# Two-layer graph network: one tile of every eighth group fetched row by row, and a second pass with 15 groups made and four gathered early

## Chip, cores and metric

The kernel runs on one core of a Trainium2 chip. The metric is the device time of one execution in microseconds, the median of several runs. Six actors matter: TensorE (PE, with its weight loads PEld), VectorE (DVE), ScalarE (ACT), GpSimd (POOL), which issues gathers, SyncE (SP), which issues plain copies, and the 16 DMA engines that all of them share.

## What is computed

A graph of N = 6250 nodes with 96 features and E = 100000 edges sorted by destination. Two layers, each with a residual and a normalization:

```
h    = concat(x[src], edge_attr)                      # E x 128
msg  = gelu(h @ mW1 + mb1) @ mW2 + mb2
gate = sigmoid(gelu(h @ gW1 + gb1) @ gW2 + gb2)
agg  = segment_sum(msg * gate, dst, N)
x1   = layernorm(x + layernorm(x + mlp(concat(x, agg))) ...)
# layer 2 (GCN), deg = segment_sum(edge_weight, dst) + 1
norm = deg[src]**-0.5 * edge_weight * deg[dst]**-0.5
out  = segment_sum((x1 @ W)[src] * norm, dst, N) + self loop + b
return layernorm(x1 + out)
```

## The kernel before

**Tiling.** Edges are cut into tiles of 128 and groups of TG = 8 tiles (1024 edges); there are NG = 98 groups. Nodes are cut into NB = 49 blocks of 128. As the edges are sorted by destination, a group's destinations lie in a window of W = 80 nodes, so its sums are one accumulated product with a one-hot of 80 columns (`ps_win`), which VectorE adds into `acc1`.

**Pass 1** (`step1` on each engine, one step a group). GpSimd gathers x[src] of a tile with one indirect DMA (L430), eight a group, into a ring of eight `rows` buffers; it waits for `s_xt`, the transposes of the group eight earlier. TensorE transposes the eight tiles (L520, `transposes`), ScalarE copies them out (L769), TensorE multiplies (L543, L546), ScalarE applies Gelu (L784), VectorE makes gate, values and one-hot (L1034 to L1126), TensorE sums the window (L493). Every second step also finishes one node block: update, both normalizations, and x_nat[:, b], the scaled input of layer 2, written by VectorE (L1203) and sent to the table `x1s_table` in HBM by ScalarE's queue (L854).

**Dense groups.** Gathering is dear on GpSimd, so in pass 2 only some groups are gathered. For the others TensorE multiplies x_nat, which is in SBUF, with a matrix B of 128 x (49 blocks x 12 nodes) for each of the group's eight tiles: B[i, (block, node)] holds the weight of each edge whose source is row i of the block. B is itself the product of two one-hots made by VectorE (`hots`, L1133 and L1137). 40 groups are dense: 24 are *stored* (kind P): their B is made in pass 1 beside the other work, two tiles each step (`pair_hot`, `pair_cells` L571, `pair_copy` L824), and SyncE stores the pair to `b_table` in HBM (L406, 96 pairs of 600 KB) and loads it again in pass 2 (L393). The pair's buffer is one of two: ScalarE's copy waits on `s_stored` for the store two pairs earlier. 16 groups are *built* (kind B): their B is made in pass 2 (`dense2` on VectorE, `cells2` L625 on TensorE, L829 on ScalarE).

**Pass 2** (`usual2`). It runs in turns, one dense group a turn. `second_pass` (L54) says which gathered groups are added in the same turn: one in a stored turn, two in a built one, one more in three turns, and a 41st turn with the last two gathered groups alone. On TensorE a stored turn q is: sums over blocks 0 to 5 (L645), turn-over of the sums of q-1 (L715, if that was a stored one), blocks to 11, placing of q-1's sums (L721), blocks to 32, gathered groups (L730), node matmuls of the output parts ready after q-1 (L692), the other blocks. A built turn is: 16 cells with turn-over, placing and outputs among them, then gathered groups, then sums over 49 blocks (L642). VectorE in turn q: the node one-hot (L1242), one-hot and weights of each gathered group (L1034, L1043), the one-hots of the next group if it is a built one (two halves of L1133 x4 and L1137), the output parts ready after q-1 (`block2`, L1294 to L1309), then the window additions of turn q (L1281), for which it waits for the placing, in TensorE's turn q+1. Node blocks are finished in parts of three; a part is ready when the last group that adds to it has been added. GpSimd's gathers of pass 2 wait for all of `x1s_table` (`s_xsw`) and then for the window addition of the group eight earlier (`s_acc2`).

**Order around the change.** Each engine runs its program in order. A function `run_pass` (L290) is called twice by TensorE, ScalarE and VectorE: each time the engine reads one number and branches to the usual case or to a general one. In pass 1 SyncE's queue holds only the pair stores, behind the loads of the start (2.4 MB each for x_t and x_nat).

## Time and profile before

| | us |
|---|---|
| median of 3 runs (1638.93 to 1643.31) | 1641.12 |
| the profiled execution | 1641.43 |
| its span | 1639.6 |
| TensorE busy | 1435.3 (88%) |
| VectorE busy | 1143.4 (70%) |
| GpSimd busy | 1178.4 (72%) |
| ScalarE busy | 559.8 (34%) |

Pass 1 takes about the first 1008 us of the span, pass 2 the rest. Busy counts time inside instructions; a queue that issues without pause (GpSimd: 0.94 us in a gather and 0.30 us between two) shows 75% busy and is full. The order in time and the waits say more than the shares.

### The profile page before, as it was taken

The numbers are of one execution on the slowest core, as the hardware profiler recorded it, in microseconds if no ns is written. First come the engines' busy times: TensorE is split into PE (matmuls) and PEld (weight loads), VectorE is DVE, ScalarE is ACT, GpSimd is POOL, SyncE is SP. The second block draws the span as 40 slices with busy tenths as digits, with TensorE's granted clock in tenths as the row PEclk, the third lists the DMA queues.
The fourth block names the chain that finished last, engine by engine and source line by source line (L and its number), as shares of the span: only waits on it lengthen the run. The fifth ranks groups of instructions, "written<-read, shape, count | busy, mean of one in ns | idle before, by whom it ended". The sixth has DMA issues, their size and how long they took to land.

```text
span 1639.6 us, 31556 instructions
## 1 busy us (share of the span) xinstructions
PE 1435.3 (88%) x11180; PEld 1273.6 (78%) x11181; DVE 1143.4 (70%) x3201; ACT 559.8 (34%) x985; POOL 1178.4 (72%) x1257
## 2 busy tenths in 40 slices
PE   3526999999999999999999987899999999998996
PEld 2415878787878778787877776799998989887986
DVE  5314889888988888889888887444654556555543
ACT  1103545454544545454544443111111111212110
POOL 7777777777777777777777770677777777777771
PEclk8767999999999999999999999999999999999997
DMA  3423444344444444444444443454544435353530
GB/s 106 123 67 109 133 120 131 115 134 116 134 117 126 124 127 125 115 134 118 133 116 127 122 116 115 130 173 125 168 143 126 165 104 167 101 191 102 196 112 19
DMA packets 80039, 205.95 MB, mean 126 GB/s; under 512 B 39325, under 2 KB 40893, under 8 KB 76703
## 3 DMA queue, kind: packets, MB, share of 16 engines
q1 hardware_dynamic: 28688, 127.68, 20.5%
q0 software_dynamic: 39808, 61.22, 17.4%
q10 hardware_dynamic: 11376, 14.90, 3.1%
q8 instruction: 95, 1.56, 0.4%
q14 instruction: 72, 0.59, 0.1%
HBM read 139.91 MB, written 63.80 MB: 124 GB/s over the span
## 4 chain that ended last, share of the span: by engine, by line
DVE 37%; PE 34%; DVEq 14%; issue 7%; DMA 3%; another core or an unknown queue 2%; POOL 2%; ACT 1%; ACTq 0%; POOLq 0%
DVE shared L1137 8%; PE ps_bt L642 8%; PE ps_win L730 5%; PE ps_xt L645 5%; PE ps_hid L645 4%; DVE logit L1126 4%; DVE shared L1133 3%; DVE edges L1102 3%; DVEq L1125 3%; PE ps_hid L625 3%; PE ps_xt L625 3%; DVEq L1049 2%; DVE prod L1123 2%; DVEq L1100 2%
## 5 line engine op out<-in xcount | busy, mean ns | idle before, releaser
L430 POOL DMA_INDIRECT rows<-in_x_nat,idx x782 | 740.5, 947 | 243.0 <-issue 237.0
L430 POOL DMA_INDIRECT rows<-x1s_table,idx x462 | 436.0, 944 | 184.6 <-issue 139.9
L546 PE MATMUL ps_hid<-w,edges 128*128 128x192 f32 x1568 | 325.2, 331 | 0.0
L546 PEld LDWEIGHTS ps_hid<-w,edges 128*128 128x128 f32 x1568 | 272.2, 194 | 14.3 <-issue 1.3
L1137 DVE TENSOR_TENSOR shared<-cell,ps_fix 128x1200 f32<-128x1200 f32 (+1 forms) x128 | 218.3, 1706 | 0.0
L784 ACT ACTIVATE edges<-ps_hid 128x768 f32<-128x768 f32 x196 | 159.1, 812 | 172.1 <-PE ps_hid L546 171.1
L1281 DVE TENSOR_TENSOR acc<-acc,ps_win 96x80 f32 x98 | 22.9, 234 | 240.2 <-PE ps_win L721 217.0
L493 PE MATMUL ps_win<-hot,edges 128*98 128x80 f32 x1568 | 156.1, 254 | 28.7 <-DVE acc L1051 28.6
L493 PEld LDWEIGHTS ps_win<-hot,edges 128*98 128x98 f32 x1568 | 148.8, 170 | 40.8 <-DVE edges L1102 39.1
L520 PE MATMUL ps_xt<-ident,rows 128*96 128x128 f32 x784 | 108.9, 284 | 71.9 <-ACT shared L824 40.2
L520 PEld LDWEIGHTS ps_xt<-ident,rows 128*96 128x96 f32 x784 | 89.2, 131 | 87.1 <-ACT shared L824 50.4
L543 PE MATMUL ps_hid<-b_split,ones_b 128*128 128x384 bf16 x392 | 129.9, 331 | 7.6 <-DVE step L998 5.9
L824 ACT ACTIVATE shared<-ps_hid 128x600 f32<-128x600 f32 x96 | 64.4, 671 | 189.6 <-PE ps_hid L571 189.6
L1034 DVE TENSOR_TENSOR hot<-dst_rel,ps_fix 128x640 f32<-128x640 f32 x156 | 126.6, 811 | 0.1
L769 ACT ACTIVATE edges<-ps_xt 96x1024 f32<-96x1024 f32 x98 | 100.0, 1020 | 72.3 <-PE ps_xt L520 68.6
L571 PE MATMUL ps_xt<-shared 128*128 128x300 f32 x384 | 114.4, 421 | 4.3 <-DVE shared L1137 4.3
L571 PE MATMUL ps_hid<-shared 128*128 128x300 f32 x384 | 116.2, 425 | 0.9 <-ACT edges L784 0.9
L730 PE MATMUL ps_win<-hot,rows 128*96 128x80 f32 x928 | 95.5, 264 | 21.6 <-DVE hot L1043 19.9
L1133 DVE TENSOR_SCALAR shared<-ps_fix,src_low,weight 128x128 f32<-128x128 f32 x320 | 112.6, 401 | 1.9 <-issue 1.9
L730 PEld LDWEIGHTS ps_win<-hot,rows 128*96 128x96 f32 x928 | 92.2, 180 | 26.4 <-issue 24.9
L824 ACT ACTIVATE shared<-ps_xt 128x600 f32<-128x600 f32 x96 | 64.4, 671 | 118.1 <-DVE edges L1102 53.4
L1126 DVE TENSOR_REDUCE logit<-prod 128x8 f32<-128x768 f32 x98 | 93.4, 953 | 7.2
(157 smaller groups left out, 2241.8 us busy)
## 6 DMA issues: line engine op xcount, KB each, us to landing
b_table<-shared SPq DMA_DIRECT2D x96, 600.0 KB, 3.4
edges<-b_table SPq DMA_DIRECT2D x12, 2400.0 KB
wide<-b_table SPq DMA_DIRECT2D x12, 2400.0 KB
rows<-in_x_nat,idx POOLq DMA_INDIRECT x782, 2.7
edges<-in_edge_t ACTq DMA_DIRECT2D x96, 128.0 KB
rows<-x1s_table,idx POOLq DMA_INDIRECT x462
wide<-in_x_t SPq DMA_DIRECT2D x1, 2376.5 KB
out_nodes<-y SPq DMA_DIRECT2D x49, 48.0 KB
```

Source lines behind the costliest of these rows:

```text
L430: nc.gpsimd.indirect_dma_start(out=rows[slot][:, k, :], out_offset=None, in_=table, in_offset=bass.IndirectOffsetOnAxis(ap=idx[:, TG * g + ...
L493: mm = nc.tensor.matmul(ps_win[0:rws, 0:W], lhs[:, k, :], hot[u][:, k, :], start=(k == 0), stop=(k == TG - 1))
L520: mm = nc.tensor.transpose(ps_xt[m // 4][0:ND, P * (m % 4):P * (m % 4 + 1)], rows[v][:, m, :], ident[:, :])
L546: mm = nc.tensor.matmul(ps_hid[j][:, HC * q:HC * (q + 1)], feat[u][:, P * m:P * (m + 1)], w1[:, :], start=False, stop=(q == 1))
L571: mm = nc.tensor.matmul(ps_pair[i][:, m, 0:HW], pair_low[n % 2][:, i, :], pair_place[n % 2][:, 2 * i + m, :], start=True, stop=True)
L642: mm = nc.tensor.matmul(ps_bt[0:TW, 0:ND], unit_b[d % 2][:, TW * c:TW * (c + 1)], x_nat[:, c, :], start=(c == 0), stop=(c == NB - 1))
L645: mm = nc.tensor.matmul(raw_sums(d), x_nat[:, c, :], unit_b[d % 2].rearrange("p (k x) -> p k x", k=TG)[:, :, WD * c:WD * (c + 1)], start=( ...
L730: mm = nc.tensor.matmul(ps_win[0:ND, W * col:W * (col + 1)], rows[i % SLOTS][:, k, :], hot[i % 2][:, k, :], start=(k == 0), stop=(k == TG ...
L784: nc.scalar.activation(flat(hid[u][:, 4 * half:4 * half + 4, :]).rearrange("p (j c) -> p j c", j=2), ps_pair[1][:, :, 0:2 * HC], ACT.Gelu) ...
L1126: nc.vector.tensor_reduce(logit[u][:, :], prod[:, :, :], AX, ALU.add).then_inc(s_logit, 1)
L1133: nc.vector.tensor_scalar(low[:, i, :], places_ps[:, 0:P], src_low[:, TG * d + k:TG * d + k + 1], weight[:, TG * g + k:TG * g + k + 1], AL ...
L1137: return nc.vector.tensor_tensor(place, cells.to_broadcast(shape), places_ps.rearrange("p (o w) -> p o w", o=1).to_broadcast(shape), ALU.i ...
```

## The change

1. **Row fetches in pass 1.** In the groups 15, 23, ..., 95 (11 of them) the last tile isn't gathered by GpSimd. SyncE copies its 128 rows one at a time from x_nat in HBM into one of two buffers (`far`), with the row's number read from SBUF into a register (eight numbers a read): 16 rows after each of the first 88 pair stores. TensorE's transposes of these groups wait for `s_far` too.
2. **Early gathers.** SyncE also copies each of the first 43 finished node blocks to a second table `x1s_early`, whose 44th block is zeros. After pass 1's gathers GpSimd gathers the groups 1, 4, 6, 7 from it, with the source number cut off at the zero block. What these groups take from the last six blocks is computed as for a dense group, with 72 columns instead of 600 (`early_cells`, `early_sums`, `early_placed`), after the sums of the first two built turns.
3. **Turns.** One built site (group 44) becomes a gathered group: 39 turns, 15 built, 59 gathered groups (four of them early). The gathered groups of each turn come from a table `TAKES`; there is no 41st turn. In the last turn they follow all the sums, and turn-over and placing come after them.
4. **One branch.** `run` holds both passes inside one branch.

```diff
+LEFT_OUT = (18,)
+SITE = [i for i in range(len(SITES)) if i not in LEFT_OUT]
+EARLY = (1, 4, 6, 7)
+DONE_B = 43
+EARLY_IN = {BUILT[0]: (0, 1), BUILT[1]: (2, 3)}
+TAKES = (0, 0, 2, 2, 2, 1, 1, 2, 2, 2, 2, 2, 2, 2, 2, 0, 1, 1, 1, 1, 2, 2, 2, 0, 2, 1, 2, 0, 1, 2, 2, 1, 2, 2, 2, 2, 2, 2, 2)
+FAR = [SLOTS * k + FAR_V for k in range(1, ROUNDS)]
...
+            def far_rows(i, first, n, buf):
+                for r in range(first, first + n, FAR_LOAD):
+                    _, nodes = nc.values_load_multi_w_load_instructions(
+                        far_idx[i:i + 1, r:r + FAR_LOAD], engines=(mybir.EngineType.SP,), min_val=0, max_val=N - 1,
...
+                    for m, node in enumerate(nodes):
+                        sp.dma_start(far[buf][r + m:r + m + 1, :], t["x_nat"][ds(node, 1), :]).then_inc(s_far[buf], 16)
...
                     sp.dma_start(b_table[P * p:P * (p + 1), 2 * CELLS * v:2 * CELLS * (v + 1)], ready_b[n % 2]).then_inc(s_stored[n % 2], 16)
+                    b = n // 2 - LAG - 1
+                    if n % 2 == 0 and 0 <= b < DONE_B:
+                        sp.wait_ge(s_xs, b + 1)
+                        sp.dma_start(x1s_early[P * b:P * (b + 1), :], x_nat[:, b, :]).then_inc(s_early, 16)
+                    if n < SLOTS * len(FAR):
+                        i = n // SLOTS
+                        if n % SLOTS == 0 and i >= 2:
+                            sp.wait_ge(s_xt, FAR[i - 2] + 1)
+                        far_rows(i, FAR_ROWS * (n % SLOTS), FAR_ROWS, i % 2)
...
+                pool.wait_ge(s_early, 16 * DONE_B)
+                for i in range(NE):
+                    pool.wait_ge(s_xt, NG - SLOTS + i + 1)
+                    early_gathers(i)
                 pool.wait_ge(s_xt, NG)
...
+            def early_part(q, es):
+                for e in es:
+                    early_cells(e)
+                for e in es:
+                    early_sums(q, es, e)
+                early_placed(q, es)
...
-                        gathered_of(turn)
+                        if q < NTURN - 1:
+                            gathered_of(turn)
                         outputs(q - 1)
                         dense_sums(q, range(SUMS_AFTER, NB))
+                        if q == NTURN - 1:
+                            gathered_of(turn)
+                turn_over(NTURN - 1)
+                place_sums(NTURN - 1)
+                outputs(NTURN - 1)
```

On TensorE the node matmuls of a part (`block2`, L686) begin with `wait(pe, s_finr, b)`: the part before must have been read by VectorE.

Turns as both tables give them (kind, gathered groups, node blocks ready after the turn), where the prediction speaks of them:

```
before: 14 P 31 (13-15) | 15 P 33 | 16 B 35 37 || 19 P 43 (19-21) | 20 P 45 | 21 B 47 49
after:   4 P 2 9 (0, 1-3) | 5 P 11 | 6 B 13    || 18 P 44 (19-21) | 19 P 45 | 20 B 47 49
after:  33 P 79 81 (37-39) | 34 P 83 85 | 35 B 86 88 (40-42) | 36 P 90 91 | 37 B 93 95
```

## Rows read from the trace of the kernel before

**Rows 1.** Waits of GpSimd, whole span: us in total, times, longest.
```profile
POOL rows L430 <- issue: 376.9, 1237, 0.3
POOL rows L430 <- DMA x1s_table<-x_nat: 44.1, 1, 44.1
POOL rows L430 <- PE ps_xt L520: 3.7, 3, 3.1
```

**Rows 2.** Order in time (start, us, engine, line, operation, [idle before]): transposes, one gather.
```profile
147.55 1.04 PE L520 MATMUL ps_xt<-ident,rows 128*96 128x128 f32 x8
...
148.89 0.94 POOL L430 DMA_INDIRECT rows<-in_x_nat,idx  x1 [0.31 <-PE ps_xt L520]
...
901.23 1.04 PE L520 MATMUL ps_xt<-ident,rows 128*96 128x128 f32 x8
911.92 1.77 PE L520 MATMUL ps_xt<-ident,rows 128*96 128x128 f32 x8 [2.28 <-issue]
...
991.95 1.04 PE L520 MATMUL ps_xt<-ident,rows 128*96 128x128 f32 x8
```

**Rows 3.** Order in time: ScalarE's wait for the first pair store.
```profile
135.96 0.67 ACT L824 ACTIVATE shared<-ps_xt 128x600 f32<-128x600 f32 x1 [39.10 <-DMA b_table<-shared]
```

**Rows 4.** Order in time: SyncE's queue issues small loads at the start.
```profile
7.13 0.28 SPq L385 DMA_DIRECT2D mw<-in_mb  x1
7.46 0.31 SPq L385 DMA_DIRECT2D uw1x<-in_uW  x1
...
9.65 0.43 SPq L385 DMA_DIRECT2D ln_g<-in_ln_g  x1
```

**Rows 5.** Order in time, then the page's DMA issues (count, KB, us to landing).
```profile
494.33 0.67 ACT L824 ACTIVATE shared<-ps_xt 128x600 f32<-128x600 f32 x1 [0.39 <-PE ps_xt L571]
496.34 0.33 DVE L1203 TENSOR_SCALAR x_nat<-h_c,root,dinv 128x96 f32<-128x96 f32 x1
...
b_table<-shared SPq DMA_DIRECT2D x96, 600.0 KB, 3.4
```

**Rows 6.** Order in time: VectorE and TensorE at the switch of passes.
```profile
1030.43 1.36 DVE L1133 TENSOR_SCALAR shared<-ps_fix,src_low,weight 128x128 f32<-128x128 f32 x4 [1.91 <-issue]
1033.21 0.57 PE L645 MATMUL ps_xt<-edges,x_nat 128*96 128x96 f32 x4 [2.69 <-issue]
1035.45 0.80 PE L645 MATMUL ps_xt<-edges,x_nat 128*96 128x96 f32 x4 [1.67 <-issue]
```

**Rows 7.** Order in time: TensorE in a built turn and the stored turn after it.
```profile
1244.56 1.20 PE L625 MATMUL ps_xt<-shared 128*128 128x300 f32 x4
...
1255.82 4.49 PE L730 MATMUL ps_win<-hot,rows 128*96 128x80 f32 x32 [2.51 <-DVE hot L1043]
...
1268.52 1.69 PE L645 MATMUL ps_xt<-wide,x_nat 128*96 128x96 f32 x18
...
1274.13 1.51 PE L730 MATMUL ps_win<-hot,rows 128*96 128x80 f32 x16
...
1278.38 1.20 PE L625 MATMUL ps_hid<-shared 128*128 128x300 f32 x4
```

**Rows 8.** Order in time: VectorE beside the start of that built turn.
```profile
1242.60 1.35 DVE L1133 TENSOR_SCALAR shared<-ps_fix,src_low,weight 128x128 f32<-128x128 f32 x4
1243.88 2.64 DVE L1137 TENSOR_TENSOR shared<-cell,ps_fix 128x2400 f32<-128x2400 f32 x1
1246.62 0.77 DVE L1294 SCALAR_TENSOR_TENSOR h<-ps_bn,dinv,x1b 128x96 f32<-128x96 f32 x3
...
1253.24 0.23 DVE L1281 TENSOR_TENSOR acc<-acc,ps_win 96x80 f32 x1 [0.69 <-issue]
```

**Rows 9.** Waits of TensorE from 1050 us on: us in total, times, longest.
```profile
PE ps_win L730 <- DVE hot L1043: 19.9, 9, 4.4
```

**Rows 10.** Order in time: TensorE at the end.
```profile
1622.67 5.38 PE L730 MATMUL ps_win<-hot,rows 128*96 128x80 f32 x32 [4.44 <-DVE hot L1043]
1629.49 1.60 PE L692 MATMUL ps_bn<-w_gcn,agg_t 96*128 96x96 f32 x6 [1.45 <-ACT agg_t L868]
```

More of the change, by code:

```diff
@@ L42 @@
 STORED = [d for d in range(NTURN) if KIND[d] == "P"]
-GATHERED = [g for g in range(NG) if g not in DENSE]
-DT = NTURN * TG
+FIRST_BUILT = BUILT[0]
+EARLY = (1, 4, 6, 7)
+NE = len(EARLY)
+DONE_B = 43
+LATE_B = NB - DONE_B
+LATE_C = LATE_B * WD
+GATHERED = list(EARLY) + [g for g in range(NG) if g not in DENSE and g not in EARLY]
+DT0 = len(SITES) * TG
+DT = DT0 + NE * TG
 PAIRS = len(STORED) * TG // 2
@@ L64, in second_pass @@
     added = {g: q for q, turn in enumerate(turns) for g in turn}
+    whole = dict(place)
+    for q, es in EARLY_IN.items():
+        for g in [EARLY[e] for e in es]:
+            added[g], whole[g] = max(added[g], q), max(whole[g], place[turns[q][0]])
     parts = []
@@ L68, in second_pass @@
         needs = range(min(2 * (b + n - 1) + 3, NG))
-        parts.append((b, n, max(added[g] for g in needs), max(place[g] for g in needs) + 1))
+        parts.append((b, n, max(added[g] for g in needs), max(whole[g] for g in needs) + 1))
     return turns, place, parts
 TURNS2, PLACE, PARTS = second_pass()
-assert PAIR_AT + PAIRS == NG
+assert PAIR_AT + PAIRS == NG and not set(EARLY) & set(SITES)
+assert FIRST_BUILT == 1 and len(TURNS2[0]) == len(TURNS2[1]) == 1
 assert ND + ED == P and NB == TURNS and SLOTS % 2 == 0 and LEFT == 2
@@ L417, in end1, with early_gathers, gathers @@
                     outputs(q)
[L418 removed]
             sp.wait_ge(s_steer, 1)
             hard = sp.value_load(steer[0:1, 3 * NG:3 * NG + 1], min_val=0, max_val=NG * NW)
+            sp.wait_ge(s_far_idx, 16)
             with sp.If(hard < 1):
                 end1()
+            with sp.Else():
+                for i in range(len(FAR)):
+                    sp.wait_ge(s_xt, FAR[i] - SLOTS + 1)
+                    far_rows(i, 0, P, 0)
         @block.gpsimd
         def _(pool):
[L427 removed]
+            def early_gathers(i):
+                for k in range(TG):
+                    nc.gpsimd.indirect_dma_start(
+                        out=rows[slot_of(i)][:, k, :], out_offset=None, in_=x1s_early,
+                        in_offset=bass.IndirectOffsetOnAxis(ap=idx_early[:, TG * i + k:TG * i + k + 1], axis=0)).then_inc(
+                            s_rows2[i % SLOTS], 16)
+            def gathers(g, slot, table, rows_sem, n):
                 last = g == NG - 1
[L429 removed]
+                elsewhere = table is not x1s_table and g in FAR
+                for k in range(TG - (REST if last else 1 if elsewhere else 0)):
                     nc.gpsimd.indirect_dma_start(
@@ L1224, in end1 @@
                 block1([], last)
-            run_pass(dve, step1, lambda b: block1a(b, False), ahead=True, even=LAG + 1, end=end1, close=close1, finish=finish1)
             def step2(k, v, easy, b):
```

296 lines of the change are left out of this document (209 added, 87 removed).

## The prediction

> **What bounds the kernel now.** I read the waits first, then the order of time. GpSimd's waits [rows 1] say that its queue issues gathers end to end: 1237 gaps of 0.3 us between descriptors, one pause of 44.1 us at the switch between the passes, and almost nothing spent on TensorE (3.7 us in 3 waits). A queue that never stops looks like the bound. The question is whether anybody waits for it, and when.
>
> Pass 1. Read the starts of a group's eight transposes [rows 2]. Group 6's stand at 147.55 and group 88's at 901.23: 82 groups in 753.7 us, 9.19 us each. GpSimd needs 8 x 1.25 = 10.0 us for a group; it was eight groups ahead at 148.89, where its last wait for TensorE ends [rows 2], and loses 0.8 us a group. Its group 89 is issued by 148.89 + 76 x 10.0 = 908.9, and there TensorE waits for the first time (911.92, 2.28 us idle). From then on TensorE follows the gathers: group 97 at 991.95. So pass 1 has two bounds: TensorE and its partners to group 88, the gathers for the last nine groups only. Before group 6 there is a third: ScalarE stands 39.1 us for the first pair store, which lands behind the big loads on SyncE's queue [rows 3].
>
> Pass 2. GpSimd again runs through, but TensorE's waits name it nowhere. They name the one-hots: 19.9 us in nine waits for L1043 [rows 9]. One long wait stands in the rows of a built turn [rows 7]: cells from 1244.56, then nothing for 2.5 us until 1255.82. VectorE shows why [rows 8]: it ends the one-hots of this built group at 1246.5, then has an output part's three node blocks (1246.62 to 1253.2, 6.6 us with the value reads behind them), then window additions, and only then the hots that TensorE wants at 1253.3. This is the pattern of five such waits (2.51, 2.18, 2.78, 3.97, 3.06 us, 14.5 together): an output part became ready, the next turn is a stored one (short) and the one after it a built one. A sixth, 4.44 us, stands ahead of the last two gathered groups [rows 10]. After such a wait 32 matmuls take 4.49 us where a quick set takes 2.87 (twice the 16 of [rows 7] gives 2.7), so each costs 1.6 us more.
>
> **The change, part by part.**
>
> (a) Row fetches. 11 of the 782 gathers of pass 1 leave GpSimd, 11 x 1.25 = 13.75 us, all after its last wait, so all are kept. Group 97's rows, landing near 989, would land near 975. TensorE on its own rhythm gets to group 97 at 901.23 + 9 x 9.19 = 983.9, not 991.95. The gain is 8.0 us; the rest of the 13.75 is slack.
>
> (b) What pays for it: SyncE issues 11 x 128 = 1408 copies of one row, 16 after each pair store, with two register reads of eight numbers. Small copies on this queue stand in [rows 4]: one row to one partition takes 0.28 us and the next starts 0.33 us after it; a 128-partition copy takes 0.43 (0.48 with its gap). No row shows a copy with an address from a register, nor a register read on SyncE. Over two groups (18.4 us) SyncE has two pair stores (0.65), one early store (0.42), and 32 rows at c each. With c = 0.33 that is 11.7 us, at 0.48 16.4 us; it fills the 18.4 us at c = 0.54. I take c = 0.45, nearest to the one-row copies and with an allowance for the reads: 15.5 us, it fits. The new wait for s_xs on even groups stands ahead of 16 rows and the next pair store: pair copies end at 495.0, x_nat is written at 496.67 [rows 5], so 1.7 us of idle, inside the 3 us left. The next pair store may then be late by 1 to 2 us; a store lands in 3.4 us [rows 5] and its buffer is wanted a whole group later, so nobody waits. Cost 0, cover about 5 us of lateness. Priced outward: a little over c = 0.54 each extra 0.01 us costs 0.3 us per two groups, 44 times.
>
> The Trainium skill (DMA: Bandwidth & Descriptors, Rules for kernel authors) speaks against this edit: many small transfers should be coalesced, since under 64 KB one pays mostly overhead. The same page (Latency and other measured facts) puts the floor of a register read at about 600 ns; four of them in two groups would be 2.4 us, and with c = 0.33 for the copy alone, by estimate, SyncE would have 14.1 us of work: still inside.
>
> (c) The start. One load of row numbers, one store of zeros, some 25 small operations on VectorE, 0.1 to 0.2 us each. All lie ahead of the 39.1 us stall [rows 3] and vanish in it. Cost 0; without that cover up to 4 us.
>
> (d) The 43 early stores are SyncE's (in (b)). The four early groups (32 gathers, 40 us) fall in the 44.1 us pause of [rows 1]: GpSimd ends pass 1 near 972, the early ones near 1012, and the others start when x1s_table has landed. Free. They shorten GpSimd's pass 2, which nobody waits for: worth 0 as such.
>
> (e) One branch instead of two. At the switch VectorE idles 1.91 us on issue before its half of the first built group (1030.43) and TensorE 2.69 us before the rest of the sums (1033.21), then 1.67 us more (1035.45); the built group's cells follow that row's matmuls, near 1036 [rows 6]. With no second branch VectorE has the one-hots ready near 1032.5 (1028.5 + 1.36 + 2.64), and TensorE starts the cells then, near 1032.7. Gain 3.3 us (bounds 0 and 4.4).
>
> (f) Pass 2, TensorE. A built turn costs 8.7 us of cells and 8.4 us of sums, as 1244.56 to 1255.82 less the wait, and 1255.82 + 4.49 to 1268.52 with 0.2 us of overlap show [rows 7]; one goes: -17.1. One more gathered group comes: +1.4 (1.51 us for 16 matmuls at 1274.13, 1.35 net of the overlap). The early parts: for each of four groups 16 short matmuls (72 columns: 1.2 us scaled from the 16 of 80, 2.1 by the eight 128-column ones of [rows 2], 1.04 us), 12 of the sums (1.05 us by 8.4 for 98), one placing (0.2): 2.5 to 3.4. In each of two parts TensorE also waits for VectorE between first and second group (about 1.7 to 2), and for two copies of ScalarE (about 1). 8.2 us a part, 16.4 together (bounds 11 and 19).
>
> (g) Where the stalls go. I wrote out both turn tables and looked for the pattern. VectorE's terms from a turn's start: placing 2.35, additions 0.41 each, node 0.2, hots 1.6 each, one-hots of a built group 8.0 (twice 1.35 + 2.64), output part 6.6 [rows 8]. A stored turn takes TensorE 5.6 us to its gathered sums (1268.52 to 1274.13), 1.35 for each of n, 0.8 for an output part, 2.9 for the rest (1278.38 is the next turn) [rows 7]; a built one wants its first hot at 8.75. Check on before, with one gathered group in the stored turn: VectorE 2.35 + 0.8 + 0.2 + 1.6 + 8.0 + 6.6 = 19.55, TensorE 10.65; so VectorE is 8.9 into the built turn, plus two additions, node and hot 11.5, wait 2.8; measured 2.5, so I take 0.4 off each. In the new table the pattern stands before turns 20, 35 and 37: one wait of 2.5 and, with two gathered groups in the stored turn, two of 3.4; with 1.6 to 1.7 of slow matmuls each, 14.4 us. Turn 10 gives 0.5. And a new one: output parts 0 and 1 to 3 are both ready at turn 4. The second part's matmuls wait for VectorE to have read the first (s_finr), and VectorE gets there only after the built one-hots of turn 6: 2.35 + 1.2 + 0.2 + 1.6 + 8.0 + 0.9 = 14.2 after the start of turn 5, TensorE is there at 7.2. 7.0 us plus 1.7 slow. New stalls 23.6; old ones leave 14.5 + 5 x 1.6 = 22.5.
>
> (h) The end. The last two gathered groups now follow the sums directly; the 4.44 us wait and 2.5 us of slow matmuls go (5.38 for 2.87, [rows 10]): -6.9. Turn-over, its two copies, the placing and a third addition now stand between these sums and the last node matmuls: 4.0 us where 1.4 are (1628.05 to 1629.49), while 1.6 ahead of them go: +1.0.
>
> Sum: pass 1 -8.0, switch -3.3, pass 2: -17.1 + 1.4 + 16.4 + 23.6 - 22.5 - 6.9 + 1.0 = -4.1. Together -15.4, from the profiled execution's 1641.4 us (span 1639.6, 1.8 outside) to 1626; the median of the runs is 0.3 us less. Forecast 1626 us.
>
> **The rivals.**
> A, SyncE becomes the bound of pass 1, the one that ends slower. A copy with a computed address, and its part of the reads, costs more than 0.54 us. Then the pair stores come late, ScalarE waits for s_stored, and TensorE behind it. With a row priced as the dearest small copy (0.48) plus 0.1 for address and reads, c = 0.58: 1.1 + 18.6 = 19.7 against 18.4, 1.3 x 44 = 57 us, in all about 1683. For it: 84% of the queue's time is filled at c = 0.45, and no row has the form. Against: the one-row copies are the cheap ones. At the threshold the change turns from gain to loss within 0.02 us of c (0.015 x 32 x 44 = 21 us).
> B, GpSimd was the bound of pass 2 after all, and its relief counts in full: its 438 gathers start near 1022 and end at 1569, where before 462 from 1030.0 end at 1607.5; 38 us sooner, and the end follows: about 1603. For it: no pause in [rows 1], TensorE near 97% busy. Against: [rows 9].
> C, nothing comes through: TensorE's rhythm in pass 1 slows by 0.1 us a group, as SyncE's copies share issue and DMA rings with ScalarE's (8 us), and the early parts cost their upper bound or their waits bring the slow clock: 1640, between 1636 and 1646.
>
> **How the numbers follow.** Forecast and what lies near it (1608 to 1636): 0.62. A: 0.18. B: 0.07. C: 0.13. The bounds of (e), (f), (g) move the forecast by +-9 us. The low end is 1606, so that B is left out. The high end, 1650, takes in C and the mildest part of A; outside lie most of A and of B, some 2 in 10. About 0.3% (4.9 us) is what a measurement of this kernel can tell from no change. Faster by more: forecast and B, 0.69. Within: C but for 0.01, 0.12. Slower by more: A and that 0.01, 0.19.
>
> **What would show it.** (a) No wait of TensorE for rows after group 88, group 97's transposes near 984, and GpSimd's pass 1 ended near 972. (b) SyncE's row copies 0.3 to 0.45 us apart and ScalarE without waits for b_table; many such waits would be A. (e) Cells about 3.3 us nearer to the last stores. (f) Two parts of about 8 us. (g) One TensorE wait of 7 us before the node matmuls in turn 5, and three of 2.5 to 3.5 before turns 20, 35, 37's gathered sums. (h) No wait before the last gathered pair. I am wrong if the rhythm of 9.19 us moves, or if TensorE waits for rows in pass 2.

## The result and the profile after

The changed kernel takes **1687.3 us** (median of 4 runs, 1683.1 to 1692.4) against 1642.0 us (4 runs) of the kernel before. The ratio is 1.028, with a 95% interval of 1.025 to 1.031: slower by 45 us. The forecast was 1626 with a range of 1606 to 1650, so it was wrong in sign. What came is rival A, put at 0.18 and priced at 1683.

In some runs below every kernel, the kernel before included, takes half as long again, so a time that stands beside a kernel before of 2485 to 2516 us is compared with that one alone.

The profiled execution took 1692.4 us (span 1690.5), the longest of the four; before it was 1641.4 (1639.6). Read in the order in which the prediction read the kernel before, it says this.

Waits first (engine, line, waited for: us in total, times, longest). This is the view of rows 1 and 9, of the changed kernel:

```profile
ACT shared L949 <- DMA b_table<-shared: 178.2, 69, 38.0
PE ps_xt L609 <- ACT shared L949: 99.4, 57, 36.8
...
POOL rows L506 <- DMA x1s_table<-x_nat: 27.0, 1, 27.0
POOL rows L506 <- DVE acc L1473: 15.9, 6, 10.9
POOL rows L506 <- PE ps_xt L609: 9.3, 15, 5.0
```

ScalarE's copy of a pair's cells (L949) waited for a pair store once, 39.1 us, in the kernel before [rows 3]. Now it waits 69 times. The first wait is that old one (38.0 us); the other 68 share 140 us, some 2.1 each. TensorE stands behind it 57 times. GpSimd, which was to be relieved, now waits for TensorE more often than before [rows 1].

Then SyncE's queue, in order of time, over two groups:

```profile
480.41 0.36 SPq L461 DMA_DIRECT2D b_table<-shared  x1
480.83 0.42 SPq L465 DMA_DIRECT2D x1s_early<-x_nat  x1
483.56 7.35 SPq L455 DMA_DIRECT2D shared<-in_x_nat  x16
490.96 0.36 SPq L461 DMA_DIRECT2D b_table<-shared  x1
492.64 7.29 SPq L455 DMA_DIRECT2D shared<-in_x_nat  x16
499.98 0.36 SPq L461 DMA_DIRECT2D b_table<-shared  x1
```

From one even pair store to the next are 19.57 us (19.45 around 430 us), with no pause: each store is issued some 0.05 us after the last row copy. The gaps ahead of the row copies (2.3 us from the end of the early store to 483.56, 1.3 us from the end of the pair store to 492.64) are register reads; a third and a fourth read stand inside the batches of sixteen. Grouped by line (operation, count: ns least/median/most, first and last start):

```profile
L451 SPq TENSOR_LOAD <-shared x176: 562/943/2238, 133.1 to 987.6; - x176
L455 SPq FUSED_REGOPS  x1408: 37/37/48, 133.7 to 991.7; - x176
L455 SPq MOVE shared<-in_x_nat x1408: 29/29/38, 133.8 to 991.8; - x176
L455 SPq DMA_DIRECT2D shared<-in_x_nat x1408: 224/228/628, 133.9 to 991.8; - x176
```

The page's chain of work that ended last names the same queue, which had no part worth a word in it before: SPq has 47% of the span, of it L455 (the row copies) 25% and L451 (the reads) 11%.

TensorE's transposes (rows 2's view) and the stall of turn 5:

```profile
149.33 1.04 PE L609 MATMUL ps_xt<-ident,rows 128*96 128x128 f32 x8
...
1036.86 1.04 PE L609 MATMUL ps_xt<-ident,rows 128*96 128x128 f32 x8
...
1172.05 1.56 PE L779 MATMUL ps_bn<-w_gcn,agg_t 96*128 96x96 f32 x6 [6.09 <-DVE h L1486]
```

Group 6 to group 97 take 887.5 us, 9.75 us a group: half of SyncE's 19.5. Before, group 97 stood at 991.95 [rows 2], so **44.9 us of the loss are made in pass 1**. From group 97's transposes to the end of the span are 653.6 us, where the kernel before has 647.7: 6.0 more before rounding. The two are the whole difference of the spans (50.9). The 6.0 can't be laid to the change: a run below with the same pass 2 (one read of sixteen) has 645.9 us there.

### The profile page after: what moved, and what is told of

Read it like the earlier page. It is cut to its first block, busy times and chain, and to the rows that moved or that the text cites. A ratio compares the mean times of both kernels' runs of the same rounds, so it can differ in the third digit from the quotient of the medians.

```text
span 1690.5 us, 36100 instructions
## 1 busy us (share of the span) xinstructions
PE 1449.3 (86%) x11184; PEld 1282.5 (76%) x11185; DVE 1155.8 (68%) x3266; ACT 552.9 (33%) x986; POOL 1177.4 (70%) x1254
## 4 chain that ended last, share of the span: by engine, by line
SPq 47%; PE 29%; issue 13%; DVE 8%; DVEq 2%; DMA 1%; ACT 0%; ACTq 0%
SPq L455 25%; SPq L451 11%; PE ps_bt L731 7%; SPq L435 6%; PE ps_win L817 4%; PE ps_hid L734 4%; PE ps_xt L734 4%; PE ps_xt L714 3%; PE ps_hid L714 3%; SPq L461 2%; DVE shared L1289 2%; SPq L432 2%; SPq L465 1%; DVE shared L1285 1%; DMA edges<-b_table 1%
## 5 line engine op out<-in xcount | busy, mean ns | idle before, releaser
L506 POOL DMA_INDIRECT rows<-in_x_nat,idx x771 | 730.9, 948 | 241.8 <-issue 230.0
L506 POOL DMA_INDIRECT rows<-x1s_table,idx x438 | 414.2, 946 | 174.2 <-issue 131.4
L1289 DVE TENSOR_TENSOR shared<-cell,ps_fix 128x1200 f32<-128x1200 f32 (+1 forms) x126 | 213.0, 1691 | 0.0
L949 ACT ACTIVATE shared<-ps_xt 128x600 f32<-128x600 f32 x96 | 64.4, 671 | 198.2 <-DMA b_table<-shared 178.2
L949 ACT ACTIVATE shared<-ps_hid 128x600 f32<-128x600 f32 x96 | 64.4, 671 | 168.2 <-PE ps_hid L660 166.6
L1251 DVE TENSOR_SCALAR ps_fix<-squash 128x8 f32<-128x8 f32 x98 | 16.2, 165 | 129.8 <-ACT squash L928 128.5
L817 PEld LDWEIGHTS ps_win<-hot,rows 128*96 128x96 f32 x944 | 91.1, 175 | 17.7 <-issue 16.2
```

The lines of the kernel that those rows point to most:

```text
L506: nc.gpsimd.indirect_dma_start(out=rows[slot][:, k, :], out_offset=None, in_=table, in_offset=bass.IndirectOffsetOnAxis(ap=idx[:, TG * g + ...
L817: mm = nc.tensor.matmul(ps_win[0:ND, W * col:W * (col + 1)], rows[slot_of(i)][:, k, :], hot[i % 2][:, k, :], start=(k == 0), stop=(k == TG ...
L1289: return nc.vector.tensor_tensor(place, cells.to_broadcast(shape), places_ps.rearrange("p (o w) -> p o w", o=1).to_broadcast(shape), ALU.i ...
```

## The experiments

The two theories at the start: **S**, SyncE's queue needs 19.55 us of issue for two groups where TensorE wants 18.4 (2 x 9.19), and everything waits for the pair stores behind it. Against it stand **D** (the small transfers themselves are in the way on the DMA rings) and **P** (the new pass 2 costs, and the late stores are a symptom). Where nothing else is said, the median of the kernel before beside a run is 1642.3 to 1643.8 us.

### Without the row fetches

```diff
-                elsewhere = table is not x1s_table and g in FAR
+                elsewhere = False
-                    if n < SLOTS * len(FAR):
+                    if False:
```

> The kernel after without the row fetches: GpSimd gathers all eight tiles of every group again; the early stores, the one branch and the new pass 2 stay. Theory S (SyncE's queue needs 19.55 us for two groups of pass 1 where TensorE wants 18.4, and everything waits for the pair stores): without the 32 row copies and four register reads SyncE has some 2 us of work in two groups, the 69 waits of ScalarE for b_table fall back to one, group 6 to group 88 run at 9.19 us a group, group 97's transposes stand near 992, and the time is the 1687 less some 45: 1638 to 1648. What is left against 1642 of the kernel before is the work of the new pass 2 (its trace says about +6 behind group 97, and -1 at the switch). Rival P (the new pass 2 is what costs, by more DMA traffic or slow matmuls, and the late stores are a symptom): over 1665.

Measured: 1647.7 us (10 runs; ratio to before 1.003, 1.0013 to 1.0047). ScalarE waits for b_table once:

```profile
ACT shared L947 <- DMA b_table<-shared: 38.4, 1, 38.4
```

and group 97's transposes stand near where they did before (in order of time):

```profile
993.71 1.04 PE L607 MATMUL ps_xt<-ident,rows 128*96 128x128 f32 x8
```

P falls: with the whole of the new pass 2 and all early stores kept, 40 of the 45 us are gone. What is left, 4.7 us, is the price of everything in the change but the rows, which gained nothing.

### The same 1408 copies from fixed rows

```diff
-                    _, nodes = nc.values_load_multi_w_load_instructions(...)
-                    for m, node in enumerate(nodes):
-                        sp.dma_start(far[buf][r + m:r + m + 1, :], t["x_nat"][ds(node, 1), :])...
+                    for m in range(FAR_LOAD):
+                        sp.dma_start(far[buf][r + m:r + m + 1, :], t["x_nat"][r + m:r + m + 1, :])...
```

> The kernel after, with the same 1408 copies of one row at the same places, but from fixed row numbers: no register reads and no computed addresses on SyncE. This changes what is computed: the last tile of eleven groups gets other rows. Theory S: what costs is SyncE's time for reads and computed addresses; 32 copies at 0.28 to 0.33 us and 1.25 us of stores are 10.2 to 11.8 us of the 18.4, so the rhythm is 9.19 again, group 97 near 984 (no wait for the gathers either), 1630 to 1640. Rival D (the small transfers themselves are in the way: 1408 more descriptors beside the stores and gathers on the DMA rings, so that stores land late): nothing gained, near 1687, with ScalarE's waits for b_table still there while SyncE's queue stands idle.

Measured: 1641.7 us (10 runs; 0.9997, 0.9986 to 1.0007), just above my 1630 to 1640: group 97 comes at 988.17, not near 984. ScalarE waits for b_table once (36.7 us). SyncE's queue over a bit more than two groups:

```profile
480.82 0.35 SPq L462 DMA_DIRECT2D x1s_early<-x_nat  x1
481.21 4.71 SPq L452 DMA_DIRECT2D shared<-in_x_nat  x16
486.27 0.35 SPq L458 DMA_DIRECT2D b_table<-shared  x1
486.67 5.59 SPq L452 DMA_DIRECT2D shared<-in_x_nat  x16
496.53 0.35 SPq L458 DMA_DIRECT2D b_table<-shared  x1
498.99 0.35 SPq L462 DMA_DIRECT2D x1s_early<-x_nat  x1
```

Now the queue idles (492.3 to 496.5). D falls: the same number of transfers of the same size, on the same queue, costs nothing. So the 45 us are what SyncE does to find the addresses. This edit changes one more thing, as the rows copied are now numbers 0 to 127 and not scattered ones; that their place in HBM isn't the cost rests on two runs below, one in which half the scattered rows cost nothing and one in which a mere reordering gives 25 us. Sixteen copies take 4.7 to 5.6 us, 0.30 to 0.35 each, as the one-row copies at the start [rows 4].

### One read of sixteen numbers

```diff
-FAR_ROWS, FAR_LOAD = P // SLOTS, 8
+FAR_ROWS, FAR_LOAD = P // SLOTS, 16
```

> The kernel after with one register read of sixteen numbers after each pair store, where it has two reads of eight. Everything else is the same. Theory S with a price for each read instruction (0.96 us for the read between two batches of eight rows): 19.55 - 2 x 0.96 = 17.6 us in two groups, under the 18.4; the pair stores are in time, rhythm 9.19 to 9.25, group 97 near 984 to 990, 1632 to 1642. Rival V (a read costs by the values it brings, not by the instruction): 19.5 us in two groups as before and near 1687. Rival D (the small transfers are in the way): near 1687 as well, but with SyncE idle between its batches.

Measured: 1688.7 us (4 runs; 1.0285, 1.0257 to 1.0313): no gain, and rival V is right.

```profile
L451 SPq TENSOR_LOAD <-shared x88: 1285/2254/2602, 132.7 to 983.7; - x88
```

In order of time (the view ends at 500 us and cuts the last batch off after 15 of its 16 copies):

```profile
481.31 0.42 SPq L465 DMA_DIRECT2D x1s_early<-x_nat  x1
484.17 6.83 SPq L455 DMA_DIRECT2D shared<-in_x_nat  x16
491.05 0.36 SPq L461 DMA_DIRECT2D b_table<-shared  x1
494.04 6.02 SPq L455 DMA_DIRECT2D shared<-in_x_nat  x15
```

Half the reads, each more than twice as long (2.25 us for 0.94; at their least 1.29 for 0.56). A read costs by the values it brings, 0.07 to 0.08 us each at the least and 0.12 to 0.14 in the middle, not by the instruction. The least times carry this: all reads of sixteen stand behind a store and only half of those of eight do, so the medians don't compare like with like. My expectation had this wrong; theory S's own number was right, 19.6 us for two groups.

### Half the rows

```diff
-FAR = [SLOTS * k + FAR_V for k in range(1, ROUNDS)]
-FAR_ROWS, FAR_LOAD = P // SLOTS, 8
+FAR = [SLOTS * k + FAR_V for k in range(3, ROUNDS, 2)]
+FAR_STEPS = 2 * SLOTS
+FAR_ROWS, FAR_LOAD = P // FAR_STEPS, 8
```

> The kernel after with row fetches for every sixteenth group only (31, 47, 63, 79, 95): eight rows and one read after each pair store, 640 rows in all. Theory S: 16 x 0.40 + two reads (2.3 + 1.2) + 1.25 = 11.2 us in two groups, far under the 18.4. GpSimd keeps 5 x 1.25 = 6.25 us, so it falls behind TensorE later: group 97 near 986, ScalarE's waits for b_table gone, 1632 to 1642. Rival D (the small transfers are in the way, in proportion to their number): half of the 45 us stays, near 1665.

Measured: 1643.0 us (10 runs; 0.9999, 0.9986 to 1.0011), 1 us over my range. No proportion: half the rows cost nothing (and gain nothing), all of them 45 us. That is a threshold. ScalarE's wait for b_table is again one (38.8 us), and group 97's transposes stand at 988.57. A batch of eight computed rows is in the trace by itself:

```profile
481.08 0.35 SPq L468 DMA_DIRECT2D x1s_early<-x_nat  x1
482.38 3.21 SPq L458 DMA_DIRECT2D shared<-in_x_nat  x8
486.53 0.35 SPq L464 DMA_DIRECT2D b_table<-shared  x1
487.95 3.14 SPq L458 DMA_DIRECT2D shared<-in_x_nat  x8
```

Its reads of eight, grouped by line:

```profile
L454 SPq TENSOR_LOAD <-shared x80: 537/757/1116, 132.8 to 854.9; - x80
```

Start to start the batches of eight give 0.42 us a row ((3.14 - 0.23) / 7), 0.07 to 0.12 above the fixed ones. The two register operations of a row, 37 and 29 ns, are 0.066 of the 0.42.

### The read ahead of the store

The same instructions in another order: the first read of a step stands before the wait for the pair, so that it comes behind row copies and not behind a store.

```diff
+                    read = far_read(n // SLOTS, FAR_ROWS * (n % SLOTS)) if n < SLOTS * len(FAR) else None
                     sp.wait_ge(s_pair_out, 2 * n + 2)
```

> The kernel after, with the first of the two register reads of a step moved ahead of the wait for the pair's cells and of its store; the second read stays between the eight-row batches. The same instructions, in another order. Since the run with one read of sixteen numbers took as long as with two of eight (2.25 us for one against 0.94), theory S is kept with a changed price: a read costs by the number of values, and more when it stands directly behind a store of 128 partitions (2.1 us behind the early store, 1.1 behind a pair store, 0.8 to 0.96 behind eight row copies). Expected by it: all four reads of two groups then stand behind row copies, 4 x 0.9 = 3.6 us instead of 4.9, SyncE needs 12.8 + 3.6 + 1.3 = 17.7 to 18.3 us for two groups where TensorE wants 18.4, and it just fits: ScalarE's waits for b_table mostly gone, 1638 to 1655. Rival R (the time is not the read's: SyncE's queue takes work at one rate set by the copies already in its ring, and a read only shows that): the order changes nothing, 19.5 us in two groups and near 1687.

The same kernel again, twice:

> The same kernel as in the run with the read moved first, again: on the chip of that call every kernel took half as long again (the kernel before 2516 us), TensorE's clock stood at 0.82 and releases came late on all engines, so that it doesn't tell the two theories apart. Expected as there: by theory S with reads that cost more behind a store, four reads of about 0.9 us, 17.7 to 18.3 us of SyncE in two groups where TensorE wants 18.4, 1638 to 1655; by rival R (the order changes nothing) 19.5 us in two groups and near 1687.

> The kernel after with the first register read of a step moved ahead of the pair store, a third time: in two calls every kernel took half as long again, the kernel before too. Expected in the state of the earlier runs, as before: by theory S with reads that cost more behind a store, four reads of 0.8 to 0.9 us, 17.7 to 18.3 us of SyncE in two groups where TensorE wants 18.4, 1638 to 1655; by rival R (the order changes nothing) 19.5 us in two groups and near 1687.

Measured: 1662.0 us (4 runs; 1.0129, 1.0108 to 1.0151) in the third, between my two cases. In the first two it was 2603 and 2601 us against 2516 and 2514 of the kernel before, 1.034 both times. ScalarE still waits for b_table 50 times in the third, 117.2 us with the first wait's 38.4. SyncE's queue in order of time, and its reads grouped by line:

```profile
480.20 0.36 SPq L465 DMA_DIRECT2D b_table<-shared  x1
480.76 7.50 SPq L458 DMA_DIRECT2D shared<-in_x_nat  x16
489.12 0.36 SPq L465 DMA_DIRECT2D b_table<-shared  x1
489.53 0.42 SPq L469 DMA_DIRECT2D x1s_early<-x_nat  x1
490.16 8.03 SPq L458 DMA_DIRECT2D shared<-in_x_nat  x16
499.04 0.36 SPq L465 DMA_DIRECT2D b_table<-shared  x1
```

```profile
L450 SPq TENSOR_LOAD <-shared x176: 541/787/952, 132.8 to 957.3; - x176
```

Rival R falls: order alone gives 25 us. The median read fell from 0.94 to 0.79 and the longest from 2.24 to 0.95, so **a read behind a 128-partition store takes longer than one behind row copies**: in the changed kernel's two groups 2.09 us behind a pair store and an early store, 1.11 behind a pair store alone, and 0.78 for each of the two behind row copies. Two groups take 18.84 us, not the 17.7 to 18.3 expected, because the row copies took up some of what the reads gave back (0.43 and 0.47 us each in the two batches, by (7.50 - 0.23 - 0.79) / 15 and (8.03 - 0.23 - 0.79) / 15). This run is the calibration that the sum lacked. With 88 groups, 44 times two, and 1641.7 us for a SyncE that fits (fixed rows):

| kernel | SyncE, two groups | over 18.38, x 44 | measured over 1641.7 |
|---|---|---|---|
| after | 19.57 | 52 | 46 |
| one read of sixteen | 19.6 | 54 | 47 |
| read ahead of the store | 18.84 | 20 | 20 |
| half the rows | fits | 0 | 1 |

A cost that is zero below the mark and about 44 times the excess above it: theory S holds with its numbers, to within 7 us. Why the two large cases come out 6 and 7 us under the sum isn't shown.

### One computed row in eight, and reads without copies

The first keeps all reads, but seven of eight copies have fixed row numbers; the second keeps the reads and drops all copies.

```diff
+                        row = ds(node, 1) if m == 0 else slice(r + m, r + m + 1)
```

> The kernel after with all its register reads, but of each eight row copies only the first takes its row from a register; the other seven have fixed row numbers. This changes what is computed: seven of eight rows of the last tile of eleven groups are other rows. It prices the reads apart from the computed addresses. (The run meant to do that with no copies at all showed none: reads whose values nobody uses were left out by the compiler.) By theory S: 32 copies at 0.31 us as in the run with fixed rows (9.9), four reads at what they cost in the kernel after (4.9), 1.3 of stores: 16.1 us in two groups, under the 18.4, so pass 1 runs at 9.2 us a group and the time is 1638 to 1645. If the reads were longer only because the copies between them were slow, they fall to 0.6 us each and SyncE to 13.6 us. If the reads are the whole cost (a computed address costs nothing): 19 us and near 1685.

> The same kernel as in the run with one computed row address of eight, at the normal pace. Seven of eight rows of the last tile of eleven groups are other rows. By theory S: 32 copies at 0.31 us (9.9), four reads at what they cost in the kernel after (4.9), 1.3 of stores, 16.1 us in two groups, under the 18.4: 1638 to 1645. If the reads were long only because of the computed copies between them: 0.6 us each and 13.6 us. If the reads are the whole cost: 19 us and near 1685.

> The kernel after with SyncE's register reads but without its row copies (GpSimd gathers all eight tiles, as in the run without row fetches). In half of the steps a step's sixteen numbers are read as two times eight, in the other half as one times sixteen. If a read's price is its own (by values): about 0.55 to 0.6 us for eight and 1.1 to 1.3 us for sixteen, the least times that the traces with copies show. If a large part of it is waiting for the copies and stores before it: the least times stay, but the medians fall far below the 0.94 and 2.25 us that were seen with copies. If behind a store it costs more whatever else is there: 1.1 us and more for the first of each pair. In any case SyncE has under 8 us of work in two groups, and the time is that of the run without row fetches, 1643 to 1650.

Reads without copies: 2535.9 us against 2515.7 (1.008), one run, and no read in its trace. Nothing in that kernel uses the values, which is the likely reason; so it is the run without row fetches over again and prices nothing. One computed row: 2544.5 us against 2514.3 (1.012) and 2507.8 against 2486.0 (1.009). The first of the two stood beside the second run of the read ahead of the store (2601.4, 1.034), so these two compare. One computed row in eight costs little more than the run without copies (1.008), as theory S has it, but that is a single run. A batch of the kernel with two computed rows in sixteen, in order of time:

```profile
615.25 6.00 SPq L456 DMA_DIRECT2D shared<-in_x_nat  x16
```

and one of the kernel with sixteen:

```profile
604.54 13.40 SPq L458 DMA_DIRECT2D shared<-in_x_nat  x16
```

With one read inside the batch in both (medians 0.78 us), 14 computed addresses more cost 7.4 us there; the other full batches between 580 and 680 us take 5.7 to 7.1 us in the one trace and 11.7 to 14.3 in the other. So the reads are not the whole cost. Why a computed copy takes so much longer in this trace than the 0.42 us above isn't shown. The split of the 45 us between reads and addresses rests on the traces of the earlier runs and was not tried by itself.

### Output parts one turn later

Two kernels test the reading that TensorE waits where VectorE has an output part and a built group's one-hots in one short stored turn. The first is the run with half the rows plus the shift below (four parts, among them that of turn 5):

```diff
+LATER = {1: 5, 19: 19, 37: 34, 40: 36}
-        parts.append((b, n, max(added[g] for g in needs), ...))
+        parts.append((b, n, max(LATER.get(b, 0), max(added[g] for g in needs)), ...))
```

> The run with half the rows (1643.0), with four output parts made ready one turn later than their inputs allow: the parts from block 1 (turn 5), 19 (turn 19), 37 (turn 34) and 40 (turn 36). Nothing is left out. By the reading that TensorE waits where VectorE has an output part and the one-hots of a built group in one short stored turn, and in turn 5 because two parts became ready in one turn: the waits of 6.1, 2.4, 4.4 and 4.2 us go, and with each the slow matmuls behind it (1.4 to 1.6 us): -22 us if nothing is late in their place, 1621 (1616 to 1630). Rival (the delayed part only moves the wait to the turn in which it now falls, since VectorE's total work sets the pace there): within 5 us of 1643.

> The same kernel as in the run with four output parts one turn later, again, since on the chip of that call every kernel took half as long again. Expected as there against the run with half the rows (1643.0): the waits of 6.1, 2.4, 4.4 and 4.2 us go with their slow matmuls, 1621 (1616 to 1630); rival (the wait only moves with the part): within 5 us of 1643. On the slow chip it was 1.1% behind the kernel before, which speaks for the rival or for something that only shows where releases are late.

> The same kernel as in the two runs with four output parts one turn later, now that the kernel before runs at 1642 us again. Expected against the run with half the rows (1643.0): the waits of 6.1, 2.4, 4.4 and 4.2 us go with their slow matmuls, 1621 (1616 to 1630); rival (the wait only moves with the part): within 5 us of 1643.

> The same kernel as in the three runs with half the rows and four output parts one turn later (from blocks 1, 19, 37, 40), at the normal pace. The kernel before with five parts later came to 1627: its five waits for one-hots were gone, but TensorE then waited 8.1 us in 7 places for the gathered rows of pass 2, which GpSimd issues without a pause. The new pass 2 has 24 gathers fewer there (438 for 462) and starts them no later, so it has 30 us of room. Expected: the waits of 6.1, 2.4, 4.4 and 4.2 us go with their slow matmuls, no wait for rows comes, 1621 (1616 to 1630), ahead of the 1627: then the early parts are worth what they cost only once VectorE is out of the way. Rival (the waits only move): within 5 us of 1643. Rival G (the gathers bind here too): 1627 or more, with TensorE waiting for rows.

Each time it came out at 2512 to 2545 us, 1.011, 1.010, 1.010 and 1.011 of the kernel before beside it (2485 to 2516). Neither 1621 nor a rival can be read from that: from 1480 us on TensorE waits 0.9 to 3.4 us for one-hots in these four traces, but only 6.8 us in the run without copies, which has the same pass 2 without the shift, so there was little to gain. Whether the new pass 2, with its 24 gathers fewer, keeps what the old one loses to them (below) stays open.

The second is the kernel before, with its own pass 2, half the rows, and five parts later (`LATER = {13: 15, 19: 20, 28: 27, 34: 32, 40: 37}`):

> The kernel before, with two things only: the last tile of every sixteenth group from 31 on fetched row by row by SyncE (640 rows, eight and one read a pair store, as in the run with half the rows), and five output parts (from blocks 13, 19, 28, 34, 40) ready one turn later. Pass 2 has its 16 built groups, two branches and no early parts. Expected: pass 1 gives 3 to 4 us (group 97 at 988 instead of 992, as the two runs with cheap rows showed), and the five waits of rows 9's one-hots go, 14.5 us, with 1.6 us of slow matmuls each: 1642 - 3.5 - 22 = 1617 (1612 to 1628). Against the run with parts later on the new pass 2 it tells whether leaving out a built group for two early parts was worth anything: by the traces so far the new pass 2 gives nothing (its stretch behind group 97 is 645.8 to 653.6 us in five runs, 647.7 in the kernel before).

> The same kernel as in the run of the kernel before with half the rows and five output parts one turn later, again, for the same reason. Expected as there: 3 to 4 us from the rows, 22 us from the five waits and the slow matmuls behind them: 1617 (1612 to 1628). On the slow chip it was 0.4% ahead of the kernel before. If the waits only move, some 1638.

> The same kernel as in the two runs of the kernel before with half the rows and five output parts one turn later, at the normal pace. Expected: 3 to 4 us from the rows, 22 us from the five waits and the slow matmuls behind them: 1617 (1612 to 1628). If the waits only move, some 1638.

These three gave 0.996, 0.995 and 0.996 (2506, 2501 and 2474 us against 2516, 2514 and 2486). The fourth:

> The same kernel as in the three runs of the kernel before with half the rows (640, by SyncE) and five output parts one turn later, at the normal pace. Expected: 3 to 4 us from the rows, 22 us from the five waits and the slow matmuls behind them: 1617 (1612 to 1628). If the waits only move, some 1638. In the slow state it was 0.4 to 0.5% ahead of the kernel before.

Measured: **1627.0 us** (5 runs, 1626.6 to 1630.1; ratio 0.991, 0.989 to 0.992). It beats both kernels, by 17 and by 60 us, though with 10 us less than expected. Its trace tells most of it. TensorE's waits from 990 us on, and in order of time the longest for rows and for one-hots:

```profile
PE ps_win L764 <- DMA rows<-x1s_table,idx: 8.1, 7, 3.8
PE ps_xt L679 <- issue: 5.6, 2, 3.5
PE ps_win L764 <- DVE hot L1077: 5.5, 4, 4.6
```

```profile
1360.28 2.85 PE L764 MATMUL ps_win<-hot,rows 128*96 128x80 f32 x16 [3.77 <-DMA rows<-x1s_table,idx]
1609.07 5.38 PE L764 MATMUL ps_win<-hot,rows 128*96 128x80 f32 x32 [4.58 <-DVE hot L1077]
```

The five waits for one-hots that stood in the middle of pass 2 are gone (of the 19.9 us of [rows 9] only the last one's 4.6 and three of 0.3 are left), and a wait that no row of the kernel before showed has come in their place: for the **gathered rows**, 8.1 us in seven places. GpSimd issues its 462 gathers of pass 2 from 1028.9 to 1605.2 without a pause, as it did in the kernel before (1030.0 to 1605.6); there the end of the span was 34 us behind the last one, here it is 20. From group 97 (989.38) to the end are 635.9 us for 647.7: 11.8 of the 22 expected. Rival B, that GpSimd was the bound of pass 2 after all, was no fact of the kernel before, but it is what comes next there.

## Why the prediction was wrong, point by point

**The step that failed is (b), by the size of one term: SyncE's cost of a fetched row, c, which was put so low that SyncE's queue fitted.** It asked the right question, named the right queue, and had the threshold at c = 0.54 us a row. It took c = 0.45, and the traces give (19.57 - 1.25) / 32 = 0.57. Of the 0.12 too little, 0.09 is the copy itself: 0.42 to 0.43 where 0.33 stood for a copy with a fixed address. The rest is the reads: 4.9 us in two groups (19.57 less 32 x 0.42 and 1.25), 0.15 a row, where the allowance was 0.12. Rival A's c was 0.58 and its time 1683. The mechanism of A is what the traces show; that its time came so near is in part luck, since its 57 us for pass 1 were 11 too many (1687.3 less 1641.7 is 46) and the 1626 under them 16 too few.

The reason given for 0.45 was "nearest to the one-row copies". That choice compared the shape of the transfer and left out that both things which no row showed, the address and the read, could only add. Nothing could be under 0.33, and 0.33 was the base of the sum. The prediction also had 0.54 and 0.58 side by side and the price of each 0.01 from there on (0.3 us per two groups, 44 times, some 13 us), and still gave the other side 0.18.

The Trainium skill (DMA: Bandwidth & Descriptors, Latency and other measured facts) gives about 600 ns as the least for a register read. The trace agrees for the least (0.56), but the median of reads of eight values is 0.94, and up to 2.24 behind a store. The estimate from that page, 2.4 us of reads in two groups, was half of the 4.9 found. Another page of the Trainium skill, which the prediction didn't weigh (Runtime: NRT & Kernel Launch, Instruction fetch mechanics), says that such loads cost about 200 ns a register even in bulk, for loads from HBM. The traces agree in kind: sixteen values cost twice what eight do, at 70 to 140 ns each from SBUF. By its figure, as an estimate, the 32 values of two groups would be 6.4 us. The rule of the Trainium skill that many small transfers should be coalesced (DMA: Bandwidth & Descriptors, Rules for kernel authors) came out right here for another reason than the page's: the transfers didn't cost, as the run with fixed rows shows (1641.7 us), but the instructions to find their addresses.

**(a)** Where SyncE fits (here the run with fixed rows), TensorE indeed no longer waits for rows at the end of pass 1, and GpSimd's last gather of pass 1 starts at 973.7 (foretold 972). But group 97's transposes came to 988.17, not 983.9. Two small things were left out. Group 96 stands at 976.82 and group 97 11.35 us behind it, as in the kernel before (11.36): 9.19 was the wrong last step by 2.2. And **(c)**, the start, isn't free: the first pair store's end, and group 6 with it, is later in the six traces of kernels with the new pass 2 that stand beside 1642 us: group 6 at 148.97 to 150.60 for 147.55, 1.4 to 3.1 us. The rows are worth 6.0 us (1647.7 less 1641.7), not 8.0.

**(d)** Right: the early gathers ran in the pause, and nothing shows that they were worth anything as such. In the run with half the rows GpSimd even waits 15.1 us for VectorE in pass 2.

**(e) to (h), the new pass 2.** Forecast -7.4 us. In those six traces, group 97 to the end is 645.9 to 653.6 us, 649.9 in the mean, against 647.7: +2.2, so 9.6 are to be explained. The built turn is gone as foretold: the rows of cells cover 133.8 us (mean of the six) where they covered 141.3, and those of the 49-block sums 127.7 where they covered 136.9, together 16.6 for 17.1 (+0.5). What was too small stands elsewhere:

```profile
1044.71 1.93 PE L829 MATMUL ps_xt<-shared 128*128 128x72 f32 x16
1047.57 1.11 PE L829 MATMUL ps_hid<-shared 128*128 128x72 f32 x8 [0.93 <-DVE shared L1306]
1049.21 1.11 PE L829 MATMUL ps_hid<-shared 128*128 128x72 f32 x8 [0.53 <-DVE shared L1306]
1050.16 2.22 PE L839 MATMUL ps_bt<-x_nat,wide 128*96 128x96 f32 x24
1052.80 0.56 PE L848 MATMUL ps_win<-edges 96*96 96x80 f32 x4 [0.42 <-ACT edges L1046]
...
1090.90 4.09 PE L839 MATMUL ps_bt<-x_nat,wide 128*96 128x96 f32 x24
...
1196.73 3.51 PE L819 MATMUL ps_win<-hot,rows 128*96 128x80 f32 x23 [1.93 <-DVE hot L1197]
...
1625.23 1.60 PE L781 MATMUL ps_bn<-w_gcn,agg_t 96*128 96x96 f32 x6 [2.71 <-ACT agg_t L993]
```

These are rows of the run with half the rows (the view cuts turn 10's 32 matmuls at 1196.73 off after 23; they take 4.67 us). The first early part takes 8.5 us (1044.71 to 1053.20), the 8.2 foretold. The second takes 11.2, since its 24 sums run 4.09 us instead of 2.22 behind two waits. Together 19.7, over the upper bound of 19, and 20.1 in the mean of the six; +3.7.

The switch gave 1.2 us in the changed kernel (group 97 to the first built cells 42.9 for 44.1 us) and up to 3.5 in others, 2.5 in the mean, for 3.3 (+0.8): without the second branch the cells wait 1.4 to 3.1 us for VectorE's one-hots instead. Turn 10's wait was 1.9 with slow matmuls, not 0.5: +3. Those of turns 35 and 37 were 4.2 and not 3.4: +1.7.

The end gave 4.5 us instead of 5.9: +1.4. From the last sums to the last node matmuls it gave 6.4 (12.6 us before, 6.2 now), a little more than foretold, though these matmuls wait 2.71 us for ScalarE where 1.45 stood [rows 10]. But behind VectorE's last instruction the span goes on for 4.4 us in the mean where it was 2.5, and why the last output stores take longer isn't shown.

Turn 5's wait was 0.9 shorter than foretold. Together 10.2 us for the 9.6; as the same pass 2 took 645.9 us in one trace and 653.6 in another, the single terms can't be held to be exact. The table of stalls itself held in its main places: 6.09 us in turn 5 (foretold 7.0), 2.4 in turn 20 (2.5), none before the last gathered pair.

**The rivals.** A came. B is the bound behind the bound. C's time, 1640, is what the change would have given had SyncE fitted (1641.7), and half of C's mechanism came: the early parts cost their upper bound and more. The other half did not: the rhythm of 9.2 us stayed. That the sum fits is luck, made up of the small errors above.

## What to carry to other kernels

Before work is moved to a queue that "has room", price the new form of instruction from its parts, and let every part without a row raise the base, never be averaged with it. Where the sum then stands within a tenth or two of the mark, and the mark is a rhythm that is kept 44 times, the likeliest case is not the one on the cheap side; do half of it: here half the rows cost nothing, though they gained nothing either, and all of them cost 45 us. And when a wait is taken away, look up who issues without a pause: here it was GpSimd, and waits for its rows took back 8.1 of the 22 us looked for.

## What the runs showed of the hardware

- A register read on SyncE costs by its values: eight take 0.54 to 0.56 us at the least and 0.76 to 0.94 in the middle, sixteen 1.29 and 2.25. Directly behind stores of 128 partitions a read of eight takes up to 2.24 us; with every read behind row copies none took more than 0.95.
- A one-row copy on SyncE with its row from a register comes every 0.42 us (0.43 to 0.47 in the run with the read ahead of the store), with a fixed row every 0.30 to 0.35.
- 1408 transfers of 384 bytes more, beside the stores, gathers and loads of pass 1, left its rhythm as it was (fixed rows: group 6 to group 88 in 754.1 us, before 753.7).
- In two traces with the kernel before at 2514 us beside them, a batch of sixteen computed copies took 13.4 us and the same batch with fourteen fixed rows 6.0.
